# Moving the row loads of a two-layer sequence kernel from SyncE's DMA queue to GpSimd's

## The reference

```python
W = L0_cond_weights[itok_B_0_15]                 # one 128x128 matrix per batch row
x = x + jnp.einsum('bct,bcd->bdt', x, W)
mask = jnp.arange(2048) < itok_B_8_3872[:, None] # per batch row
u = x * mask[:, None, :]
k = 2 * einsum('hn,hnl->hl', Cs, exp(dtA * arange(2048))).real   # (128 channels, 2048)
y = causal_convolution(u, k) + u * D[:, None]
x = x + y * mask[:, None, :]
```

## Time and profile before

| | kernel before |
|---|---|
| median of three runs | 2274.95 us (2273.8 to 2285.9) |
| the profiled execution | 2279.22 us |
| its span | 2277.6 us |
| PE busy | 2141.6 us, 94% |
| DVE busy | 1596.3 us, 70% |
| ACT busy | 1437.4 us, 63% |
| POOL busy | 1314.7 us, 58% |
| DMA queue q1 (SP) | 480.99 MB, 67.8% of 16 engines' span |
| DMA queue q10 (ACT) | 201.35 MB, 22.5% |
| DMA queue q0 (POOL) | 33.56 MB, 3.8% |
| row loads | 256 of 512 KB, all from SP |

### The profile page before, as it was taken

One profiled execution on the slowest core, in us unless ns is written; L12 is line 12 of the kernel. 1 busy time (PEld: TensorE's weight loads), 2 busy tenths in 40 slices (PEclk: granted clock), 3 DMA queues, 4 the chain that ended last, 5 costly groups with the idle time before them and its releaser, 6 DMA issues.

```text
span 2277.6 us, 62956 instructions
## 1 busy us (share of the span) xinstructions
PE 2141.6 (94%) x15101; PEld 1885.9 (83%) x15101; DVE 1596.3 (70%) x3359; ACT 1437.4 (63%) x4107; POOL 1314.7 (58%) x2115
## 2 busy tenths in 40 slices
PE   5877778999999999999999999899999999999999
PEld 2222226988889999998989889799999999999999
DVE  4999303777777777777777768577777777777776
ACT  4556556777767777777777777455555555555555
POOL 0995504877778878887888777333333333333330
PEclk9999998999999999999999999999999999999999
DMA  8999999999999999999999999888888888999887
GB/s 313 420 419 387 407 375 334 336 326 326 323 320 341 336 334 340 337 340 330 336 327 337 323 326 327 246 253 269 272 273 263 277 269 260 271 272 268 275 264 230
DMA packets 347685, 716.28 MB, mean 314 GB/s; under 512 B 41602, under 2 KB 172932, under 8 KB 347652
## 3 DMA queue, kind: packets, MB, share of 16 engines
q1 hardware_dynamic: 282116, 480.99, 67.8%
q10 hardware_dynamic: 55296, 201.35, 22.5%
q0 software_dynamic: 10240, 33.56, 3.8%
HBM read 395.92 MB, written 319.82 MB: 314 GB/s over the span
## 4 chain that ended last, share of the span: by engine, by line
PE 49%; DMA 28%; SPq 8%; issue 5%; ACT 4%; ACTq 3%; DVE 2%; DVEq 0%
DMA out<-decay 17%; PE bank L926 10%; PE bank L927 10%; PE bank L928 10%; PE bank L971 6%; SPq L341 5%; PE bank L963 5%; PE bank L908 4%; DMA row_x<-in_x 4%; DMA decay<-x_scratch 4%; PE bank L895 3%; ACTq L545 2%; DMA toep<-k_scratch 2%; DVE decay L829 2%; DMA x_scratch<-row_y 1%
## 5 line engine op out<-in xcount | busy, mean ns | idle before, releaser
L817 DVE TENSOR_TENSOR u_lo<-bank,u_hi 128x512 fp32r<-128x512 f32 x512 | 354.2, 692 | 201.7 <-ACT u_hi L621 198.7
L562 ACT ACTIVATE row_y<-bank 128x512 f32<-128x512 f32 x512 | 301.7, 589 | 216.1 <-PE bank L928 115.2
L829 DVE COPY_PREDICATED decay<-mask,bank 128x512 f32<-128x512 uint8 x512 | 379.2, 741 | 44.6 <-PE bank L928 36.4
L971 PE MATMUL bank<-toep,u_odd 128*128 128x128 f32 x2048 | 393.5, 274 | 0.0
L926 PE MATMUL bank<-t_hi,u_hi 128*128 128x256 f32 x1024 | 354.9, 347 | 16.3 <-DMA toep<-k_scratch 16.3
L509 POOL TENSOR_TENSOR x_lo<-row_x,x_hi 128x256 fp32r<-128x256 f32 x496 | 361.7, 760 | 0.0
L478 POOL COPY par<-table 128x71 f32 (+1 forms) x256 | 72.1, 282 | 491.0 <-DVE e_lo L812 489.8
L481 POOL TENSOR_TENSOR outer<-par 128x256 f32<-128x256 f32 x512 | 335.8, 676 | 21.1
L895 PE MATMUL bank<-row_x,w_sel 128*128 128x512 f32 x528 | 263.2, 625 | 87.2 <-DMA row_x<-in_x 52.0
L823 DVE TENSOR_TENSOR s_lo<-state,s_hi 128x128 fp32r<-128x128 f32 x768 | 295.1, 384 | 52.2 <-ACT s_hi L633 51.1
L971 PEld LDWEIGHTS bank<-toep,u_odd 128*128 128x128 f32 x2048 | 313.8, 189 | 0.0
(11 more groups left out here) (141 smaller groups left out, 5314.5 us busy)
## 6 DMA issues: line engine op xcount, KB each, us to landing
row_x<-in_x SPq DMA_DIRECT2D x256, 512.0 KB, 7.5
x_scratch<-row_y ACTq DMA_DIRECT2D x256, 512.0 KB, 7.1
decay<-x_scratch SPq DMA_DIRECT2D x256, 512.0 KB, 6.0
out<-decay SPq DMA_DIRECT2D x256, 256.0 KB, 5.5
out<-decay ACTq DMA_DIRECT2D x128, 512.0 KB, 5.6
t_hi<-k_scratch SPq DMA_DIRECT2D x256, 128.0 KB, 4.8
t_lo<-k_scratch SPq DMA_DIRECT2D x256, 128.0 KB, 4.5
b_scratch<-b_mat POOLq DMA_DIRECT2D x128, 256.0 KB, 5.7
```

Of the source, the lines that this page charges most:

```text
L817: v.tensor_tensor(u_lo[j % 2][:, blocks, :], t_bank[q][:, :].rearrange("s (k b) -> s k b", b=B), u_hi[j % 2][:, blocks, :].bitcast(fp32), ...
L829: v.copy_predicated(tile[j][:, cols], mask[:, seg * SEG + q * BANK:seg * SEG + (q + 1) * BANK], y_bank[q][:, :]).then_inc(y_taken, 1)
L971: mm(y[:, P:CHUNK], u_odd[i][:, c, :], toep[j][:, P - 1::-1], start=False, stop=True, skip_group_check=True)
```

## The change

The loads of the 124 rows of the interleaved segment are issued by POOL. SP no longer issues them, neither the three ahead of its loop nor the one in each pass. POOL issues three after its wait for `w_halved`, ahead of the first `split_row`, and then one in each pass ahead of the store of B. POOL's load waits for the same condition as SP's did, that the row four before is made. In the pass of POOL that stores B of channel k - 2, the row loaded is k - 1; SP loaded row k + 3 in its own pass of channel k. The loads signal new semaphores `row_loaded`, for which ACT's `halve_x` waits in place of `x_loaded`.

```diff
@@ -171,6 +171,7 @@
+        row_loaded = [sem(f"row_loaded{i}") for i in range(SLOTS)]
@@ -374,8 +375,6 @@
             store_kernel(2, 2)
             load_x1(0, 1, 1, 0)
-            for n in range(ROWS_FIRST, ROWS_FIRST + 3):
-                load_row(n, n % SLOTS, 1, n - B)
@@ -389,8 +388,6 @@
                     if not (isinstance(k, int) and k == 0):
                         store_x2_half(k - 1, j3, 1)
-                    if with_rows and not (isinstance(g, int) and k + 3 >= B - AHEAD):
-                        load_row(k + ROWS_FIRST + 3, j3, 1, k + AHEAD + 3)
@@ -509,12 +506,21 @@
+            def load_row(m, j):
+
+                pool.wait_ge(row_made, m * NQ + (ROWS_FIRST - SLOTS + 1) * NQ)
+                pool.dma_start(row_x[j][:, :], x[bass.ds(m + AHEAD, 1), :, SEG:2 * SEG].rearrange("a c t -> (a c) t")).then_inc(row_loaded[j], 16)
+
+            for m in range(3):
+                load_row(m, m)
             split_row(0, 0)
             for k in range(2):
                 store_b(k, k)
 
             def channels(g, with_rows):
                 for j in range(SLOTS):
+                    if with_rows or j < 1:
+                        load_row(g * SLOTS + (j - 1), (j + 3) % SLOTS)
                     store_b(g * SLOTS + (j - 2), (j + 2) % SLOTS)
                     make_e(0, g * SLOTS + j, j)
@@ -550,7 +556,7 @@
                     act.wait_ge(row_made, n * NQ - NQ)
-                    act.wait_ge(x_loaded[j], n * 4 + (16 - j * 4))
+                    act.wait_ge(row_loaded[j], m * 4 + (16 - j * 4))
```

## The result

The changed kernel takes 2403.28 us (median of four runs, 2392.94 to 2407.64) beside 2276.61 for the kernel before (median of four, the three of the table above and one more): ratio 1.0562, interval 1.0527 to 1.0596. It is 5.6% slower, about 127 us. A later measurement gave 1.0607 (1.0557 to 1.0657); it leaves out one of five executions, which took 3414.5 us at a mean granted clock of 0.558. I had forecast slower, but by 25 us, and the time lies well outside the range of 2268 to 2332.

The account below looks back on a forecast made before the run. TensorE and the DMA engines were both taken as within a few per cent of the limit, with SP's store landing deciding. Terms 0 + 0 + 0 + 18 + 7 = +25 us gave 2304, median 2300 us, range 2268 to 2332.

Parts of the forecast that it names:

- What bounds the kernel: Interleaved segment: TensorE at 8.33 us a channel and DMA engines at 99% both near the limit; 24 us lost to waits.
- (a): SP's queue: the row load's issue lies under the wait for the half store, so removing it gives 0 us.
- (b): GpSimd's queue: one more issue per channel, taken as 0.58 us, costs 0 us; at 1.16 by bytes, 12 us.
- the rival in which GpSimd becomes the bound: GpSimd's loop: a row issue over 1.06 us makes it the limit; 2373 us at 1.16 with the start; chance 0.06.
- (c): GpSimd's new wait for the row four before: load 2.2 us later in the period, ScalarE doesn't wait, 0 us.
- (d): DMA order in each turn: the later load runs beside urgent transfers; 0.15 us a turn, 18 us in all.
- cover and delay are equal within 0.1 us: DMA order: 2.8 us of other work is just used up by the load's 2.2 us shift and 0.58 issue.
- (e): The start: GpSimd sends the first row loads later; first state 5.6 us later, 7 us in all, between 4 and 11.
- a median landing of 5.6 to 5.8 us for the half stores: Sign in the trace: SP's output stores land later than 5.5 us; below 5.4 the prediction would be wrong.

Follow-up runs that it names:

- e5: Kernel before without the row loads of the interleaved segment beyond the first three, later rows computed from old contents: 2253.14 us, ratio 0.9917.
- e6: Changed kernel with SP issuing the three Toeplitz loads of the next channel ahead of the tile load: 2341.07 us, ratio 1.0308.
- e11: Changed kernel with each GpSimd row load cut to the first 128 of 1024 columns (64 KB): 2275.56 us, ratio 0.979 to a slow reference.
- e12: Changed kernel with GpSimd loading the row one earlier, without the wait, first two rows from SP: 2419.23 us, ratio 1.0408 to a slow reference.
- e13: Kernel before with the row load one issue further down SP's queue, behind the first-half store: 2377.03 us, ratio 1.0455.
- e1: Kernel before with SP's row load at the end of its pass, behind the store of the convolution kernel: 2380.27 us, ratio 1.0459.
- e8: Kernel before with SP's row load issued ahead of the second-half store instead of behind it: 2466.34 us, ratio 1.0846.
- e3: Kernel before with GpSimd issuing the row loads in the middle of its split of a row, first three from SP: 2386.40 us, ratio 1.0486.
- e14: Kernel before with ScalarE issuing the row load on its hardware queue, behind its own 512 KB store: 2332.39 us, ratio 1.0269.
- e2: Changed kernel with row loads on ScalarE's hardware queue at about GpSimd's moment, first four rows from SP: 2381.03 us, ratio 1.0464.

## Why the prediction was wrong

**What bounds the kernel: right.** TensorE at 8.33 us and the DMA engines at 99% are both at their limits, and e5 confirms that the row loads account for most of what was lost (20 of 24 us). The chain by way of store, tile load and Toeplitz loads was read right too; e6 shows that cutting its last part gives back 59 us (67 over the kernel before instead of 127).

**(a) and (b), the issues: right.** GpSimd's row issue takes 0.58 us, the lower end of my two, with 512 KB as with 64 KB (e11); 1.16 by the bytes is refuted, and with it the rival in which GpSimd becomes the bound. The rule that a GpSimd DMA takes about 3100 ns instead of 620 when it overlaps a VectorE copy (the Trainium skill, SBUF — State Buffer, "A bandwidth-pool intuition that's wrong") I had applied to the issue. The trace doesn't test it: beside 112 of the 114 issues of the changed kernel (591 ns at the longest) VectorE ran a TENSOR_TENSOR or a COPY_PREDICATED, beside the other two nothing, and a plain copy beside none.

**(c), the wait: right that nobody waits, wrong in the moment.** ScalarE never waits for the load in the steady part, and without GpSimd's wait (e12) the kernel stays slow. But the load went out 3.8 us behind the store in the median, where I had 2.9. GpSimd waits for TensorE's product, so when TensorE is late the load is too.

**(d), the order of the DMA traffic: the step that failed.** The mechanism was named there, "it then runs beside the tile load, the Toeplitz loads and the store of the next turn"; its size was taken as 0.15 us a channel and measured as 0.98, 121 us instead of 18. Three things were wrong in it. First, "cover and delay are equal within 0.1 us": I had counted 2.8 us of other work as cover, from medians of landings, and a delay of 2.2 + 0.58. The delay was 3.1, and the runs show no such cover: on the same queue, 2.4 us later costs 104 us (e13), 3.5 later costs 104 (e1), and one issue earlier, ahead of the store, 193 (e8). A load that comes late leaves the DMA engines idle for 0.67 us of each turn, against 0.09, and then stands among the urgent transfers. Second, the queue, which stays open: near SP's old moment, GpSimd's queue costs 4.9% (e3) and ScalarE's behind a long store 2.7% (e14), but neither held that moment, e3 least of all. A load that takes its share from the half store instead of standing behind it would fit; place alone costs 104 us in e1, which leaves some 22 of the 127 for the queue and the start together. Third, I left out TensorE's clock in (d): behind its waits it is at 1.2 GHz for some 66 us, up to 33 us of the loss. With 82 us of longer waits that makes up to 115 of 121.

My range's upper end for (d) was 1.58 us a turn, and the true value lies within it. But I had set it aside as improbable and capped the range at 2332. With two limits 2% apart and a load of 19% of the bytes being moved, the bound deserved weight.

**(e), the start: right in kind, and in number by luck.** Forecast: first state 5.6 us later, 7 in all. The first state now comes at 377.75 instead of 372.25, 5.5 later:

```profile
369.31 1.83 POOL L512 DMA_DIRECT2D row_x<-in_x  x3 [79.99 <-ACT w_all_hi L653]
```

```profile
373.95 1.15 ACT L560 ACTIVATE x_hi<-row_x 128x512 fp32r<-128x512 f32 x2 [4.96 <-DMA row_x<-in_x]
...
376.70 1.15 ACT L560 ACTIVATE x_hi<-row_x 128x512 fp32r<-128x512 f32 x2 [1.29 <-DMA row_x<-in_x]
377.75 0.26 ACT L636 ACTIVATE state<-bank 128x128 f32<-128x128 f32 x1
```

Three errors cancel: the issue came at 369.31, 0.9 us later than forecast, the load landed 4.6 us after it and not 6.9, and the wait for the second row, 1.29 us, did not disappear. The clock's part is there too; windows with PE busy, clock, DMA share, GB/s:

```profile
372.00:380.00 8.00, 2.92 (x17) 0.71 0.62 193
380.00:388.00 8.00, 8.00 (x47) 0.81 0.56 181
```

**A sign that misled.** I named a median landing of 5.6 to 5.8 us for the half stores as the mark of (d), and one below 5.4 as refuting me. It fell from 5.5 to 5.1, since it mixes both halves of a tile. Taken apart, the half that SP waits for went from 5.2 to 6.1 us (median, 400 to 1380 us) and the other fell from 5.7 to 4.7. SP's wait, 0.74 to 1.99 us a pass, was the mark to name.

## What to carry to other kernels

Where the DMA engines are as busy as here, 99%, the order of transfers is part of the schedule. Of all the places tried for this load, directly behind the urgent store that SP waits for, in the same queue, was the best. Taking it off a queue to save the issue (here 0.58 us that lay under a wait anyway) gives up this order. Before such a move, price the bound by moving the transfer by one issue on its old queue; that is a two-line experiment, and here it said 4.6% and 8.5% (e13, e8). Take the landing of the urgent transfer from its own issues, not from a median over a line that mixes it with others.

## What I had not expected

- An exchange of two neighbouring issues on one queue, 0.7 us, costs 193 us over 121 turns, 1.6 us each. That is near the 1.58 us that 512 KB take at 332 GB/s, but it isn't the transfer put whole in front of the store: the store's landing grows from 5.3 to 6.0 us in the mean, and it goes out 1.0 us later behind the tile load.
- Six different placements of the same load (the changed kernel, e1, e2, e3, e12, e13) all end at ratios of 1.041 to 1.061, with DMA shares of 0.92 to 0.94 in their windows.
- The busy time of the DMA engines for the same bytes isn't fixed: 8.44 us a turn before, 8.84 after. Where these 0.4 us come from is open.
- The kernel before took 2326.65 us beside e11 and e12 and 2271 to 2277 otherwise. No run settles why.
